# Combining the experts' outputs: rows sorted by token tile through an indirect store, 15 cells in place of 64 dense blocks

## The chip, the cores and the metric

The kernel runs on one core of one Trainium2 chip. The metric is device time in microseconds (us), the median of three runs. One further execution was recorded by the hardware profiler; every duration below comes from that execution.

## The reference, cut to what matters

The program is two transformer layers on 1024 tokens of width 256: attention and a low-rank mixture in layer 0, grouped attention, a shared expert and a routed mixture of 32 experts in layer 1. The change lies in the routed mixture at the end. In the reference (the wrapping removed):

```python
oh = one_hot(sel, E)                          # 1024 tokens x 4 choices, E = 32 experts
pos = (cumsum(oh, axis=0) * oh).sum(-1) - 1   # place of the choice within its expert
valid = pos < CAP                             # CAP = 32: an expert takes its first 32 tokens
xe = zeros((E, CAP, h)).at[sel, posc].add(x[tok] * valid[:, None])
g = silu(einsum('ech,ehf->ecf', xe, Wg)); u = einsum('ech,ehf->ecf', xe, Wu)
ye = einsum('ecf,efh->ech', g * u, Wd)        # 32 x 32 rows of 256
y_pair = ye[sel, posc] * (w * valid)[:, None]
out = shared.at[tok].add(y_pair)              # each row is added to its token
```

So there are 1024 slot rows of 256 values, and each is added, with its weight, to one of 1024 tokens. The layer's result is the residual X plus the attention's projection, the shared expert times a sigmoid gate, and these rows.

## The kernel before

**Engines and queues.** Each engine has its own program, written by hand, and waits on semaphores. In the last 65 us the order of the work on TensorE (PE), ScalarE (ACT) and VectorE (DVE) is the list `EXPERT_STEPS` (line 33): each engine walks the same list and does its own share of each step. GpSimd (POOL) and the queue of SyncE (SP) have orders of their own.

**Steps.** The 32 experts are 8 groups g of 4, so that a group has 128 slots. `("slots", g)` transposes the gathered token rows and ACT copies them. `("up", g)` makes both hidden halves in 16 matmuls, ACT applies silu (line 928), and DVE multiplies (line 1937) into `HE`. `("turn", g)` transposes `HE` on PE and ACT copies it to `HTE` (lines 933 and 934). `("down", g)` makes the group's 128 output rows in bank 7, and DVE copies them to `YE` (line 1940). `("sd", j)` is the shared expert's down projection of token tile j (8 tiles of 128 tokens); from tile 4 on it runs in three float32r matmuls for each product, high by low, low by high and high by high (lines 965 to 967). It needs the low parts `SDl` and `ACTl`, which DVE makes in the `("split", n)` steps (lines 1945 and 1948). `add_shared(j)` on DVE (line 1915) adds a tile to X.

**Attention of layer 1.** POOL multiplies the small attention's probabilities by the values, 32 operations of 128x256 for the eight tiles (lines 648 and 652), while the steps run. PE then transposes the result in 16 transposes (line 1446), ACT and DVE split it into high and low, and `mix_proj(j)` multiplies it by the projection, 6 matmuls for a tile.

**The combination.** `slot_mask(g)` on DVE (line 1906) compares the 1024 token numbers with the token of each of the group's 128 slots: a 128x1024 matrix of zeros and ones. ACT scales `YE` by the slots' weights into `YH` (line 911) and DVE makes the remainder `YL` (line 1910). `mix_groups(j, groups, ...)` on PE (lines 1407 and 1408) multiplies, for token tile j and each of the 8 groups, a 128x128 block of the mask by `YH` and by `YL`: 64 blocks, 128 matmuls. Tiles 0 to 3 take groups 0 to 5 within the steps ("mix", 0 to 3), as fillers between up, turn and down of group 7; the rest follows after `("down", 7)`. DVE adds each tile to X (line 1921) and SP stores it (line 525).

**Gathering.** The slots' tokens come from a table that PE, DVE and ACT build; POOL then fetches token rows by eight indirect transfers (line 638), one for each group. SP brings the experts' weights, 4 places for 8 groups.

## Time and profile before

| | us |
|---|---|
| median of 3 runs | 430.81 (430.78 to 430.83) |
| the profiled execution, its own time | 429.98 |
| its span, first to last instruction | 427.7 |
| PE busy | 422.6 (99%) |
| DVE busy | 311.3 (73%) |
| ACT busy | 248.8 (58%) |
| POOL busy | 169.2 (40%) |

How to read it: the span is what the hardware profiler saw between the first and the last instruction of the core; the execution's own time is 2.28 us more, around the span. Engines work at the same time, so that their busy times overlap. A busy PE is one with a matmul in flight, and its matmuls overlap too: the start-to-start distance is what one costs.

### The profile page before, as it was taken

What the parts mean: (1) busy time and instruction counts of PE and PEld (TensorE: products, weight loads), DVE (VectorE), ACT (ScalarE), POOL (GpSimd) and SP (SyncE); (2) the same over time, 40 slices, a digit from 0 to 9 for tenths busy, and PEclk for the clock granted to TensorE, in tenths of its full rate; (3) what the DMA queues carried; (4) which work ended last, traced back from release to release, by engine and by line L of the source; (5) the groups of instructions that cost most, each with busy time, mean ns of one, the idle gap of its engine ahead of it and who ended that gap; (6) DMA issues with size and microseconds to landing.
All of it is one profiled execution on the core that took longest, in us unless ns stands there. A gap on an engine that the chain in (4) does not pass through costs nothing.

```text
span 427.7 us, 8922 instructions
## 1 busy us (share of the span) xinstructions
PE 422.6 (99%) x3096; PEld 380.7 (89%) x3096; DVE 311.3 (73%) x913; ACT 248.8 (58%) x676; POOL 169.2 (40%) x293
## 2 busy tenths in 40 slices
PE   8999999999999999999999999999999999999997
PEld 8888889999999999999999999999997777567897
DVE  5967576787787988887877776748589995588442
ACT  4666651886868788787868687433414622463120
POOL 3232001655455455545455530101167106799100
PEclk9999999999999999999999999999999999999999
DMA  6740011501010101010000000000099952999002
GB/s 206 182 130 2 0 51 49 196 3 51 2 51 0 51 3 49 2 33 20 2 2 2 2 2 2 25 14 14 14 295 298 306 153 75 246 306 280 7 14 86
DMA packets 42026, 34.45 MB, mean 81 GB/s; under 512 B 6736, under 2 KB 40192, under 8 KB 41984
## 3 DMA queue, kind: packets, MB, share of 16 engines
q1 hardware_dynamic: 41600, 32.85, 27.1%
q0 software_dynamic: 384, 1.05, 0.9%
q8 instruction: 25, 0.41, 0.4%
q14 instruction: 17, 0.14, 0.1%
HBM read 31.80 MB, written 2.10 MB: 79 GB/s over the span
## 4 chain that ended last, share of the span: by engine, by line
PE 98%; ACT 1%; issue 0%; DVE 0%; POOL 0%; POOLq 0%; DVEq 0%
PE bank L965 22%; PE bank L966 22%; PE bank L967 22%; PE bank L1163 5%; PE bank L1175 3%; PE bank L1154 3%; PE bank L1396 2%; PE bank L1363 2%; PE bank L1407 2%; PE bank L1383 2%; PE bank L1408 2%; PE bank L1205 2%; PE bank L1053 1%; PE bank L1312 1%; PE bank L1015 1%; PE bank L1351 1%
## 5 line engine op out<-in xcount | busy, mean ns | idle before, releaser
L601 POOL TENSOR_TENSOR arena<-arena,rinv 128x384 f32<-128x384 f32 x64 | 52.9, 827 | 81.2 <-DVE rinv L1680 81.2
L965 PE MATMUL bank<-XTl,WA 128*128 128x512 f32 (+1 forms) x126 | 51.9, 412 | 0.0
L967 PE MATMUL bank<-XTh,WA 128*128 128x512 f32 (+1 forms) x126 | 49.1, 390 | 0.0
L966 PE MATMUL bank<-XTh,WA 128*128 128x512 f32 (+1 forms) x126 | 49.1, 389 | 0.0
L791 ACT ACTIVATE PT<-bank 128x256 fp32r<-128x256 f32 x64 | 24.4, 381 | 34.2 <-PE bank L1163 34.1
L1684 DVE TENSOR_TENSOR PT<-bank,PT 128x256 fp32r<-128x256 f32 x64 | 27.2, 425 | 18.8 <-ACT arena L792 18.7
L965 PE MATMUL bank<-WA,XTh 128*128 128x256 f32 x128 | 38.3, 299 | 0.0
L966 PE MATMUL bank<-WA,XTl 128*128 128x256 f32 x128 | 35.7, 279 | 0.0
L967 PE MATMUL bank<-WA,XTh 128*128 128x256 f32 x128 | 35.7, 279 | 0.0
L592 POOL CAST Q<-arena 128x128 fp32r<-128x128 f32 x64 | 18.6, 290 | 37.6 <-PE bank L967 37.6
L1672 DVE CUSTOM_DVE_ANT_0 arena<-bank,posm 128x128 f32<-128x128 f32 x64 | 18.1, 283 | 20.9 <-PE bank L967 20.8
L784 ACT ACTIVATE arena<-arena,nmax 128x256 f32<-128x256 f32 x64 | 32.4, 505 | 0.0
L594 POOL TENSOR_TENSOR Q<-arena,Q 128x128 fp32r<-128x128 f32 x64 | 29.5, 462 | 5.1
L1163 PE MATMUL bank<-ident,arena 128*128 128x128 f32 x192 | 31.4, 272 | 0.0
L797 ACT ACTIVATE arena<-bank,VC 128x256 f32<-128x256 f32 x64 | 30.0, 469 | 0.1
L967 PEld LDWEIGHTS bank<-XTh,WA 128*128 128x128 f32 x126 | 23.7, 188 | 5.3
L965 PEld LDWEIGHTS bank<-XTl,WA 128*128 128x128 f32 x126 | 23.8, 189 | 3.8
L966 PEld LDWEIGHTS bank<-XTh,WA 128*128 128x128 f32 x126 | 23.8, 189 | 3.8
L1674 DVE CUSTOM_DVE_ANT_0 arena<-bank,posm 128x256 f32<-128x256 f32 x64 | 26.9, 420 | 0.0
L782 ACT ACTIVATE arena<-arena,nmax 128x128 f32<-128x128 f32 x64 | 25.9, 405 | 1.5 <-DVE nmax L1674 1.1
L694 ACT ACTIVATE arena<-bank,bqs 128x512 f32<-128x512 f32 x16 | 18.4, 1152 | 14.0 <-PE bank L967 13.2
L1545 DVE TENSOR_SCALAR arena<-bank,bqs 128x512 f32<-128x512 f32 x16 | 17.2, 1098 | 12.7 <-PE bank L967 12.7
(345 smaller groups left out, 1471.2 us busy)
## 6 DMA issues: line engine op xcount, KB each, us to landing
arena<-in_L_ffn_Wg SPq DMA_DIRECT2D x6, 704.0 KB, 7.9
arena<-in_L_ffn_Wu SPq DMA_DIRECT2D x6, 704.0 KB, 10.1
arena<-in_L_ffn_Wd SPq DMA_DIRECT2D x6, 512.0 KB, 7.4
arena<-in_L_attn_Wk SPq DMA_DIRECT2D x8, 256.0 KB, 2.6
arena<-in_L_attn_Wv SPq DMA_DIRECT2D x8, 256.0 KB, 3.5
arena<-in_L_attn_Wo SPq DMA_DIRECT2D x1, 2048.0 KB, 9.2
arena<-in_L_ffn_Wd SPq DMA_DIRECT2D x6, 192.0 KB, 7.4
arena<-in_L_attn_Wq SPq DMA_DIRECT2D x4, 256.0 KB, 4.5
```

Of the source, the lines that this page charges most:

```text
L594: pool.tensor_tensor(QL[:, u % 3], q, QH[:, u % 3].bitcast(F32), ALU.subtract).then_inc(s_qh, 1)
L601: pool.tensor_tensor(pr, pr, r[:, :, None].to_broadcast([P, 3, P]), ALU.mult).then_inc(s_p, 1)
L782: nc.scalar.activation(Pb[i][:, 0:128], Pb[i][:, 0:128], ACT.Exp, bias=nmax[:, i, 0:1], scale=-1.0, accum_out=psumr[:, i, 0:1])
L784: nc.scalar.activation(Pb[i][:, 128:384], Pb[i][:, 128:384], ACT.Exp, bias=nmax[:, i, 1:2], scale=-1.0, accum_out=psumr[:, i, 1:2]).then_i ...
L791: nc.scalar.activation(PTH[:, u % 2], pb[2 + u % 2][:, 0:256], ACT.Copy)
L797: nc.scalar.activation(QO[:, h, b], pb[4 + u % 2][:, 0:256], ACT.Identity, bias=VC[:, 32 + h:33 + h]).then_inc(s_Oc, 1)
L965: pe.matmul(dst, wh, xl, start=start, stop=False)
L966: pe.matmul(dst, wl, xh, start=False, stop=False)
L967: return pe.matmul(dst, wh, xh, start=False, stop=stop)
L1163: ins = pe.transpose(pb[2 + u % 2][:, P * i:P * i + P], Pb[u % 3][:, P * i:P * i + P], ident[:])
L1674: nc.vector.tensor_tensor_reduce(Pb[i][:, 128:384], bank[:, 128:384], MASK, -1.0, -MASKED, ALU.add, ALU.min, nmax[:, i, 1:2]).then_inc(s_m, 1)
L1684: nc.vector.tensor_tensor(PTL[:, u % 2], pb[2 + u % 2][:, 0:256], PTH[:, u % 2].bitcast(F32), ALU.subtract).then_inc(s_Tl, 1)
```

## The change

The combination is replaced. Each slot row is given a rank: its place in an order of all slots by token tile (first all slots whose token is in tile 0, then tile 1, ...). DVE works the ranks out in four parts, `ranks(0)` to `ranks(3)`, from counts that PE makes beside the positions. ACT writes the weighted rows with the token's number as a 257th column (`YW`); POOL stores the rows of each group to a table in DRAM by an indirect store (eight "scatters"); SP loads the table back in four transfers once all eight are there. In the sorted table, block g of 128 rows and token tile j meet only along a staircase of 15 cells. For each cell i, DVE works out the tokens and makes one 128x128 mask, and PE runs two matmuls (high and low) whose bank and block are addressed by a register, loaded from `tile_of` by `value_load`. What else moves: the 8 masks of 128x1024 and the steps "mix", "high" and "low" go; DVE does tile 7 of the attention's values (`last_values`) and POOL only tiles 0 to 6, with scatters 0 to 3 ahead of tile 6; the attention's transposes come before down 7, and shared-down 6 and 7 after it; the projection starts its own sums; ACT, not DVE, empties bank 7; the zeroing of the table's first half is a 1 MB store by SP early on. Counting on PE: 16 wider matmuls in place of 36.

```diff
-                 ("mask", (4, 5)), ("split", 0), ("weigh", 0), ("down", 2), ("turn", 3), ("split", 1), ("split", 2), ("sd", 2),
-                 ("split", 3), ("down", 3),
+                 ("ranks", 0), ("split", 0), ("weigh", 0), ("down", 2), ("turn", 3), ("split", 1), ("split", 2), ("sd", 2),
+                 ("ranks", 1), ("split", 3), ("down", 3),
                  ("up", 4), ("slots", 5), ("split", 4), ("sd", 3), ("split", 5), ("turn", 4), ("split", 6), ("up", 5), ("slots", 6),
-                 ("mask", (6,)), ("down", 4), ("mask", (0,)), ("sd", 4), ("mask", (1, 2)), ("turn", 5),
-                 ("mask", (3,)), ("sd", 5), ("mask", (7,)), ("down", 5),
-                 ("high", 0), ("up", 6), ("slots", 7), ("high", 3), ("low", 0), ("sd", 6), ("turn", 6), ("low", 3),
-                 ("sd", 7), ("add", 7), ("down", 6), ("mix", 0), ("mix", 1), ("up", 7), ("mix", 2), ("turn", 7),
-                 ("mix", 3), ("down", 7)]
+                 ("ranks", 2), ("down", 4), ("sd", 4), ("ranks", 3), ("turn", 5), ("values", 0), ("sd", 5), ("down", 5),
+                 ("up", 6), ("slots", 7), ("values", 1), ("add", 5), ("turn", 6), ("down", 6), ("up", 7), ("ao", 1),
+                 ("turn", 7), ("ao", 0), ("down", 7), ("sd", 6), ("sd", 7), ("add", 6), ("add", 7)]
...
+DONE = {3: 0, 8: 1, 9: 2, 10: 3, 11: 4, 12: 5, 13: 6, 14: 7}
+PV_STEPS = [("values", j) for j in range(6)] + [("scatter", g) for g in range(4)] + [("values", 6)] + [("scatter", g) for g in range(4, GR)]
...
+            sp.dma_start(sorted_rows[0:N].rearrange("(g p) d -> p g d", p=P), ZR[:, None, :].to_broadcast([P, GR, ROW])).then_inc(s_xs, 16)
...
+            for g in range(GR):
+                sp.wait_ge(s_xg[g], 32)
+            for k in range(B):
+                sp.dma_start(YS[:, 2 * k:2 * k + 2], sorted_rows[2 * P * k:2 * P * k + 2 * P].rearrange("(g p) d -> p g d", p=P)).then_inc(s_x[k], 16)
...
+                if what == "scatter":
+                    if n == 0:
+                        pool.wait_ge(s_rk, 1)
+                    pool.wait_ge(s_ye, n + 1)
+                    pool.indirect_dma_start(sorted_rows, bass.IndirectOffsetOnAxis(ap=rank[:, n:n + 1], axis=0), YW[:, n], None).then_inc(s_xg[n], 16)
+            for g in range(1, GR, 2):
...
+                pool.tensor_tensor(y_part(g, 1), YS[:, g, 0:D], y_part(g, 0).bitcast(F32), ALU.subtract).then_inc(s_pv, 1)
...
+                if what == "down":
+                    act.wait_ge(s_dn, n + 1)
+                    act.wait_ge(s_sw1, 1)
+                    nc.scalar.activation(YW[:, n, 0:D], pb[7][:, 0:D], ACT.Copy, scale=slot_w[:, n:n + 1])
+                    nc.scalar.activation(YW[:, n, D:ROW], slot_t[:, n:n + 1], ACT.Copy).then_inc(s_ye, 1)
...
+            for g in range(GR):
+                act.wait_ge(s_x[g // 2], 32)
+                nc.scalar.activation(y_part(g, 0), YS[:, g, 0:D], ACT.Copy).then_inc(s_yr, 1)
...
-            for j in range(NT):
-                for i in range(j + 1):
-                    ins = pe.matmul(pb[6][:, E1 * j:E1 * j + E1], (trib if i == j else onesb)[:], selb[:, i],
+            for i in range(NT):
+                pe.matmul(pb[6][:, 256 + E1 * i:512].rearrange("p (j e) -> p j e", e=E1), onesb[:],
...
             def shared_down(j):
...
+                    if j == 4:
+                        pe.wait_ge(s_rk, 2)
...
                 for m in range(FC):
+                    if j >= 4 and len(tiles) < CELLS:
+                        tiles.append(pe.value_load(tile_of[0:1, len(tiles):len(tiles) + 1], min_val=0, max_val=NT - 1))
...
-                for g in groups:
-                    pe.matmul(dst, GT[g][:, ts], YH[:, g], start=start and g == groups[0], stop=False)
-                    ins = pe.matmul(dst, GT[g][:, ts], YL[:, g], start=False, stop=stop and g == groups[-1])
...
+            def values_turn(half):
+                if half == 1:
+                    pe.wait_ge(s_pd, 1)
+                    pe.wait_ge(s_pv, 25)
...
+            def cell(i):
+                pe.wait_ge(s_dm, NT + i + 1)
+                if i < GR:
+                    pe.wait_ge(s_yl, i // 2 + 1)
+                    if i % 2:
+                        pe.wait_ge(s_pv, 25 + i // 2 + 1)
+                dst = banks[:, bass.ds(tiles[i], 1), 0:D].rearrange("p a n -> p (a n)")
+                for low in range(2):
+                    rows_of = YX[:, CELLS - 1 - i:CELLS - 1 - i + NT, D * low:D * low + D]
+                    ins = pe.matmul(dst, MS[:, i], rows_of[:, bass.ds(tiles[i], 1)].rearrange("p a n -> p (a n)"),
+                                    start=False, stop=False, skip_group_check=True)
...
+            def ranks(part):
...
+                    step(nc.vector.tensor_scalar(CS[:, 1:NT + 1], TOT[:], float(CAP), None, ALU.min))
+                    step(nc.vector.tensor_tensor(SUMS[0][:, :, 16:48], CS[:, 1:NT + 1], CS[:, 0:NT], ALU.subtract))
+                    nc.vector.tensor_reduce(RS, CS, AX, ALU.add)
+                    for k in range(5):
+                        old, new, by = SUMS[k % 2], SUMS[1 - k % 2], 1 << k
+                        step(nc.vector.tensor_tensor(new[:, :, 16:48], old[:, :, 16:48], old[:, :, 16 - by:48 - by], ALU.add))
...
+                    nc.vector.tensor_copy(rank[:], T8).then_inc(s_rk, 1)
...
+                    nc.vector.tensor_copy(tile_of[:, 0:CELLS], JJ).then_inc(s_rk, 1)
...
+            def cell_tokens(i0, i1, groups):
...
+                for i in range(i0, i1):
+                    nc.vector.tensor_scalar(MS[:, i], IT, tok[:, i:i + 1], None, ALU.is_equal).then_inc(s_dm, 1)
...
+            y_low(0)
+            y_low(2)
+            cell_tokens(0, 4, 4)
+            y_low(4)
             y_low(6)
+            cell_tokens(4, CELLS, GR)
             for j in range(NT):
                 add_rest(j)
```

Of `ranks`, part 0 has 4 memsets and 8 operations of 256 to 288 columns, part 1 six of 256 and two of 4, part 2 eight of 8 to 64 (it ends in `rank`), part 3 seven of 7 to 105 up to `tile_of` and three more.

## Rows read from the trace of the kernel before

**Rows 1.** The page's head and part 1: busy us, share, instructions.

```profile
span 427.7 us, 8922 instructions
PE 422.6 (99%) x3096; PEld 380.7 (89%) x3096; DVE 311.3 (73%) x913; ACT 248.8 (58%) x676; POOL 169.2 (40%) x293
```

**Rows 2.** The page's part 4, the chain that ended last, by engine.

```profile
PE 98%; ACT 1%; issue 0%; DVE 0%; POOL 0%; POOLq 0%; DVEq 0%
```

**Rows 3.** Lines 1407 and 1408: ns min/median/max, first and last start us.

```profile
L1407 PE MATMUL bank<-YH,GT x64: 278/283/386, 399.3 to 421.2; 128*128 128x256 f32 x64
L1408 PE MATMUL bank<-OS,GT x64: 274/282/285, 399.6 to 421.3; 128*128 128x256 f32 x64
```

**Rows 4.** Timeline of PE: start us, us, engine, line, operation, tiles, form.

```profile
383.64 0.27 PE L1373 MATMUL bank<-ident,arena 128*128 128x128 f32 x1
...
386.64 0.39 PE L965 MATMUL bank<-SDl,ACTh 128*128 128x256 f32 x1
...
388.87 0.27 PE L1373 MATMUL bank<-ident,arena 128*128 128x128 f32 x1
...
407.00 1.07 PE L1383 MATMUL bank<-WAF,arena 128*32 128x256 f32 x16
408.00 1.97 PE L1446 MATMUL bank<-ident,arena 128*128 128x128 f32 x16
...
424.81 0.27 PE L967 MATMUL bank<-PJ,AOTh 128*128 128x256 f32 x1
```

**Rows 5.** Timeline of DVE; in brackets the idle time before and its releaser.

```profile
336.27 0.42 DVE L1824 TENSOR_TENSOR tmp<-tmp,sel 128x256 f32<-128x256 f32 x1
336.72 0.42 DVE L1825 TENSOR_REDUCE ws<-tmp 128x8 f32<-128x256 f32 x1
...
353.21 0.23 DVE L1887 TENSOR_SCALAR idx<-bank 128x4 uint32<-128x4 f32 x2
...
353.43 0.18 DVE L1895 TENSOR_TENSOR slot_p<-bank,slot_e 128x32 f32<-128x32 f32 x1
...
372.53 2.13 DVE L1906 TENSOR_SCALAR GT<-FRF,slot_t 128x1024 fp32r<-128x1024 f32 x2
374.59 2.20 DVE L1945 TENSOR_TENSOR SDl<-FRF,SDh 128x1536 fp32r<-128x1536 f32 x1
...
385.04 0.75 DVE L1948 TENSOR_TENSOR ACTl<-arena,ACTh 128x512 fp32r<-128x512 f32 x1 [1.12 <-ACT ACTh L945]
385.75 0.34 DVE L1937 TENSOR_TENSOR arena<-arena,bank 128x176 f32<-128x176 f32 x1
386.01 0.83 DVE L1906 TENSOR_SCALAR GT<-FRF,slot_t 128x1024 fp32r<-128x1024 f32 x1
...
425.19 0.42 DVE L1921 TENSOR_TENSOR X<-bank,X 128x256 f32<-128x256 f32 x1 [0.28 <-PE bank L967]
```

**Rows 6.** Line 525, SP's last stores: ns to issue one; us to landing.

```profile
L525 SPq DMA_DIRECT2D out<-X x8: 332/333/362, 415.0 to 425.6; - x8
```

**Rows 7.** Timeline of ACT.

```profile
389.29 0.28 ACT L933 ACTIVATE arena<-bank 128x128 f32<-128x128 f32 x1 [3.16 <-PE bank L1374]
...
408.60 0.51 ACT L911 ACTIVATE YH<-arena,slot_w 128x256 fp32r<-128x256 f32 x1 [2.49 <-DVE arena L1940]
```

**Rows 8.** Timeline of POOL: the first gather.

```profile
354.31 1.14 POOL L638 DMA_INDIRECT arena<-token_rows,idx  x1 [21.28 <-DVE idx L1887]
```

**Rows 9.** The page's part 6: issues, KB each, median us to landing.

```profile
arena<-in_L_attn_Wk SPq DMA_DIRECT2D x8, 256.0 KB, 2.6
arena<-in_L_attn_Wv SPq DMA_DIRECT2D x8, 256.0 KB, 3.5
...
arena<-token_rows,idx POOLq DMA_INDIRECT x8, 2.7
```

**Rows 10.** Windows: us, busy of the engines (x), granted PE clock, DMA share, GB/s.

```profile
427.00:427.70 0.70, 0.00 (x0) 0.00 (x0) 0.00 (x0) 0.00 (x0) 0.00 (x0) 0.61 0.00 0
```

**Rows 11.** The chain in order of time, the old counting: start us, us, line.

```profile
332.52 0.91 PE bank L1302 x36
```

More of the change, by code:

```diff
@@ L70, in sem @@
             return ctx.enter_context(nc.semaphore(name))
-        pb = [ctx.enter_context(nc.psum_tensor(f"bank{i}", [P, 512], F32)) for i in range(8)]
+        banks = ctx.enter_context(nc.psum_tensor("banks", [P, 8, 512], F32))
+        pb = [banks[:, i] for i in range(8)]
         ident = sb("ident", [P, P])
@@ L249, in program @@
         pvt = sb("pvt", [P, 256])
-        s_x = [sem(f"x_loaded{b}") for b in range(B)]
+        s_x = [sem(f"x_then_sorted_rows_loaded{b}") for b in range(B)]
         s_xb0 = sem("x_second_tile_loaded")
@@ L896, in _ @@
             nc.scalar.activation(SCp[0], SCp[0], ACT.Exp, scale=SCALE1).then_inc(s_ae, 1)
+            act.wait_ge(s_pm, 1)
+            nc.scalar.activation(TOT[:], pb[6][:, 256:512].rearrange("p (j e) -> p j e", j=NT), ACT.Copy)
             silu(3)
@@ L1465, in _, with proj @@
-            for j in range(4, NT):
-                mix_proj(j)
+                if what == "ao":
+                    values_turn(n)
+            def proj(j):
+                ts = slice(P * j, P * j + P)
+                for c in range(C):
+                    ins = mm3(pb[j][:, 0:D], AOTh[:, c, ts], AOTl[:, c, ts], PJh[:, c], PJl[:, c], c == 0, c == C - 1)
+            pe.wait_ge(s_pjl, 1)
+            pe.wait_ge(s_al, 4)
+            pe.wait_ge(s_eh, GR)
+            pe.wait_ge(s_ec, GR)
+            pe.wait_ge(s_ye, GR)
@@ L1469, in _ @@
+            for i in range(CELLS):
+                cell(i)
         @block.vector
@@ new lines, in last_values @@
+            def last_values(part):
+                j = NT - 1
+                if part == 0:
+                    dve.wait_ge(s_ap, 2)
+                for k in (0, 1) if part == 0 else (2, 3):
+                    dst = AO[:, j] if k == 0 else pvt2
+                    p, v = value_operands(j, k)
+                    step(nc.vector.tensor_tensor(dst.rearrange("p (g r d) -> p g r d", g=G1, r=4), p, v, ALU.mult))
+                    if k:
+                        ins = nc.vector.tensor_tensor(AO[:, j], AO[:, j], pvt2, ALU.add)
+                        if k == 3:
+                            ins.then_inc(s_pd, 1)
+                        else:
+                            step(ins)
@@ L1950, in _ @@
                     scores_weighed(1)
-                if what == "mask":
-                    for g in n:
-                        dve.wait_ge(s_it, 4)
-                        slot_mask(g)
-                if what == "low":
-                    for g in range(n, n + 3):
-                        y_low(g)
-                if what == "sd" and n >= 1:
+                if what == "ranks":
+                    ranks(n)
+                if what == "values":
+                    last_values(n)
+                if what == "ao":
+                    if n == 1:
+                        dve.wait_ge(s_pjh, 1)
+                        nc.vector.tensor_tensor(PJl[:], projT[:], PJh[:].bitcast(F32), ALU.subtract).then_inc(s_pjl, 1)
+                    for c in range(C):
+                        xs = slice(512 * n, 512 * n + 512)
+                        dve.wait_ge(s_ac, 2 * (1 - n) + c + 1)
+                        nc.vector.tensor_tensor(AOTl[:, c, xs], pb[ao_bank(c, n)][:], AOTh[:, c, xs].bitcast(F32), ALU.subtract).then_inc(s_al, 1)
+                if what == "sd" and 1 <= n < 6:
                     add_shared(n - 1)
```

232 lines of the change are left out of this document (141 added, 91 removed).

## The prediction

> **What bounds the kernel now.** I read the page first: PE is busy for 99% of the span [rows 1], and the chain that ended last is PE for 98% of it [rows 2]. So what PE is spared is worth its full length, as long as PE then has something else to do. What one matmul costs is read from starts, not from lengths, since matmuls overlap: shared-down of tile 4, 18 matmuls of 256 columns, runs from 386.64 to 388.87 [rows 4], 0.12 us each, while one is listed at 0.28. The combination has 128 such matmuls [rows 3]: 15.4 us of PE. The timeline of PE then shows where they lie: 48 ahead of the end of down 7 (408.00), 80 behind it, between the attention's transposes and the last matmul, which ends at 425.08 [rows 4]. Then I read DVE's timeline, because the change gives DVE work in the middle of the steps: between 372.53 and 386.01 it has one gap, 1.12 us [rows 5]. The last addition ends at 425.61 and the span at 427.7: 2.1 us for the last store [rows 5]. The sum is made against this execution (span 427.7, own time 429.98); its own time is 0.83 us under the median of the runs, so a difference in the span is added to 430.81.
>
> **What PE is spared.** 30 matmuls in place of 128: 98 times 0.12 us, 11.8 us. If nothing else changed, the span would be 416. The rest of the text is where this goes.
>
> **DVE ahead of shared-down 4.** In the new order PE may not start ("sd", 4) until `tile_of` is there, the end of `ranks(3)`'s seventh operation; before, it started at 386.64. DVE's list up to there: from 372.53 to the end of HE(5) at 386.01 are 13.48 us. Taken away: masks 4 and 5 (2.06 us, up to the start of `SDl`), two copies out of bank 7 (0.37 each, a little under the 0.42 of a like operation), the gap of 1.12, since DVE is no longer the one that waits; 9.56 us stay [rows 5]. A third copy that is gone, ahead of 372.53, lets it start at 372.2. Added: a step of 256 columns that waits for the one before it costs 0.45 us, start to start, a small one 0.21 (0.18 and its wake-up) [rows 5]. `ranks(0)`: eight of the former and four memsets of 0.1, 4.0 us; `ranks(1)`: six and two, 3.1 us. POOL multiplies the attention's values meanwhile: two masks took 1.03 us each in this stretch, one later 0.83 or less [rows 5]. So the 7.1 us are worth between 7.1 and 8.9 (times 1.25); I take times 1.2, 8.5 us, near the row of the same stretch. HE(5) is then done at 390.3; `ranks(2)` is 8 small steps, 1.7 us; the addition of tile 3 is 0.4; seven small steps of `ranks(3)` are 1.5. `tile_of` comes at 393.9: shared-down 4 starts 7.3 us late (5.5 to 7.8). Queued behind PE's wait are turn 5, shared-down 5 and all of groups 6 and 7. Half of the lateness shows earlier: HE(4) stands behind both `ranks` in DVE's list, so turn 4, which ran at 383.64 [rows 4], comes near 387.4.
>
> **From shared-down 4 to the end of down 7.** Before: 386.64 to 408.00, 21.36 us [rows 4]. Out go shared-down 6 and 7 (4.5 us) and 48 matmuls (5.8 us): 11.1 stay. In come 16 transposes, 1.7 us (1.97 less the last one's tail [rows 4]). The removed work was also cover. Before turn 6 PE now waits for silu and the multiplication, 0.1 + 0.3 + 0.34 with only the 0.2 of slots 7 beside it: 0.6; before down 6 for ACT's two copies, which start 0.42 after the turn (388.87 to 389.29) and take 0.43 together, less the turn itself: 0.7; before down 7 for ACT, which has the attention's copies in hand: 0.3 [rows 4, 5, 7]. That is 1.6 us.
>
> **Register loads.** PE does 12 `value_load`s in this stretch, one ahead of each three matmuls (0.37 us). No row shows one. Below: 0, if the sequencer works ahead and the matmuls in its queue hide it, which they cannot for the first after a wait. Above: 0.87 each, what POOL took from DVE's idx (353.44) to the start of its first transfer (354.31) [rows 5, 8]. The nearest row is the sequencer's work for one transfer on SP, 0.33 us [rows 6], less than the three matmuls that follow; I take 0.08 each to be seen, 1.0 us in all. By the Trainium skill, "DMA: Bandwidth & Descriptors", section "Latency and other measured facts", a `tensor_load` has a floor of about 600 ns; no run shown here has one. By that figure 12 loads would be 7.2 us in place of 1.0 if nothing hid them (an estimate from that page).
>
> So the end of down 7 is 393.9 + 11.1 + 1.7 + 1.6 + 1.0 = 409.3, 1.3 us later than before, although 10.3 us of PE work ahead of it are gone.
>
> **The chain behind down 7.** It is new, and each link waits for the one before. ACT's weighted copy and the token column: 0.51 and 0.2 [rows 7]. POOL's wake to an indirect transfer 0.87 [rows 5, 8], and the transfer 2.7 to landing as the gathers had; bounds 2.1 (the last store of 128 KB [rows 5]) and 3.5 [rows 9]. SP then loads four times 263 KB: like the pairs of 256 KB, 2.6 for the first and 1.3 more for the next (3.5, issued 0.4 later) [rows 9]. ACT's first high part 0.5. To here 7.4 us: 416.7. Now DVE, in its order: low part 0 (0.45), a wait for the second load (0.7), low part 2 (0.4), three small steps (0.6), four masks of 128x128 (0.2 each by size, 0.8), two low parts (0.8), three steps of up to 88 columns (0.75), eleven masks (2.2), the last cell (0.3), eight additions back to back (0.38 each, 3.0): 10.0 us, all from steps of 0.42 to 0.45 for 256 columns and 0.2 for small ones [rows 5]. Then 2.1 for the last store. End: 428.8. Meanwhile PE does shared-down 6 and 7 (4.5) and 48 projection matmuls (5.8), from 409.3 to 419.6, about when the first cells can start: this is the cover of the chain, and it ends before the chain does. The cells' register addresses, four a cell, have no row either: between 0 and 0.3 us a cell (0.33, [rows 6]); as the masks come every 0.2 us, I take 0.3 in all.
>
> **Small parts.** The counting: 36 matmuls in 0.91 us [rows 11] become 16 with twice the columns, 2304, 1.1 us at 0.12 for 256: +0.2. At nothing: the zeroing store, the three small POOL operations and ACT's copy of the totals; early on, DMA queues and POOL have idle stretches beside a PE that never stops, and if that cover were gone the store would cost its own few us once. POOL's scatters 0 to 3 start once `rank` is there, about 392.4, 1.3 us each (1.14 [rows 8] and its issue); values of tile 6 follow until about 404, just ahead of the transposes that wait for them; this costs nothing, and 1 us for each 0.25 us more a scatter.
>
> **Sum.** 428.8 + 0.3 + 0.2 = 429.3 against 427.7: +1.6 us. Median 430.81 + 1.6 = 432.4.
>
> **The rivals.** The forecast (A): the saving is spent on DVE's lateness (7.3), lost cover and the chain; 432.4, its own range 430.5 to 434.3. Chance 0.37.
>
> B, faster: DVE is less late. If the 256-column steps of `ranks` run at the 0.3 us of a one-input operation's rate (a mask of 1024 columns in 0.83 [rows 5]) or POOL does not slow them, `tile_of` comes 3 us sooner, and everything behind it moves with it: 426.3, median 429.4. It decides from 1.6 us on. For it: the chain from `tile_of` to the end has no slack, so each us counts. Against it: these steps have two inputs, like the 0.45 row. Chance 0.36.
>
> C, the clock: PE idles some 3.5 us before turn 4 and 3.6 before shared-down 4. In the trace the granted clock is 1.00 all along and falls to 0.61 on average in the last 0.7 us, some 2 us after PE's last matmul at 425.08 [rows 4, 10], so it can fall from the upper level (2.4 GHz) to the lower (1.2) in such a gap. If it does ahead of shared-down 4, its 2.2 us double: 434.6. The Trainium skill, "TensorE: Matmul & The Clock Gate", section "What's actually happening", says that the gate's default is throttled and that activity releases it; the last window agrees. Chance 0.15.
>
> D, the register loads are not hidden at all: 12 times 0.37 (0.33 [rows 6] and a wake-up) rather than 0.08, 3.5 us more: 435.9. For it: after its wait PE's queue is empty. Against it: 0.33 is less than the three matmuls behind each load. The Trainium skill's floor of a `tensor_load`, in the page and section named above, speaks for D. Chance 0.12.
>
> **How the numbers follow.** About 0.2% (0.9 us) is what a measurement of this kernel can tell from no change. B lies faster for 0.32 of its 0.36, the rest within; A lies within for 0.12 of its 0.37 and slower for 0.25; C and D are slower. Faster 0.32, same 0.16, slower 0.52. The low end takes B and adds loads and cells at 0 and DVE unhindered: 429.4 less 1.0, 0.3 and 1.4, 426.7, rounded to 426.5; the high end takes D, a scatter that lands at 3.5 (0.8) and DVE at times 1.25 (0.4): 437.1, to 437.5. Some 0.1 lies outside on either side.
>
> **What would show it.** PE idle ahead of turn 4 and of shared-down 4, the latter ended by DVE's `tile_of` near 394; the gaps between shared-down 4's threes 0.12 (loads hidden) or more; down 7 ending near 409; the last scatter landing 4.3 us behind it; DVE without a gap of more than 1 us from the first low part to the last addition; a granted clock of 1.00 through 395. The forecast is wrong if `tile_of` comes before 392, if the tail behind down 7 is under 17 us or over 22, or if the clock falls.

## The result, and the profile after

The changed kernel takes 437.87 us (437.73 to 438.28, 4 runs) where the kernel before takes 430.82 (430.78 to 431.82, 4 runs): a ratio of 1.0163 [1.0151, 1.0174], 7.0 us slower. The forecast was 432.4, its range ended at 437.5. The profiled execution of the changed kernel took 438.28 us around a span of 436.5; the working forecast a span of 429.3.

The page's head, part 1 (busy us, share, instructions) and the shares of the chain that ended last, changed kernel:

```profile
span 436.5 us, 8871 instructions
PE 418.3 (96%) x2978; PEld 371.0 (85%) x2978; DVE 317.3 (73%) x959; ACT 252.3 (58%) x693; POOL 171.1 (39%) x301
PE 87%; DVE 6%; DMA 2%; ACT 2%; issue 1%; SPq 0%; DVEq 0%
```

PE (TensorE) runs 118 matmuls fewer (98 in the combination, 20 in the counting), and its share falls from 99 to 96%: the chain is no longer PE alone [rows 1, 2]. Where PE idles is seen in its timeline (start us, us, engine, line, operation; in brackets the idle time before and its releaser):

```profile
383.68 0.59 PE L1468 MATMUL banks<-FRF,arena 128*128 128x256 f32 x2
388.47 0.48 PE L1437 MATMUL banks<-ident,arena 128*128 128x128 f32 x1 [4.20 <-DVE arena L2079]
...
389.09 2.58 PE L1427 MATMUL banks<-arena 128*32 128x352 f32 x16
...
392.21 1.78 PE L1447 MATMUL banks<-arena 128*32 128x256 f32 x16
397.55 0.57 PE L1027 MATMUL banks<-SDl,ACTh 128*128 128x256 f32 x1 [3.56 <-issue]
...
402.83 0.38 PE L1027 MATMUL banks<-SDl,ACTh 128*128 128x256 f32 x1
...
403.50 0.38 PE L1027 MATMUL banks<-SDl,ACTh 128*128 128x256 f32 x1
...
414.57 1.07 PE L1447 MATMUL banks<-WAF,arena 128*32 128x256 f32 x16
416.55 0.38 PE L1027 MATMUL banks<-SDl,ACTh 128*128 128x256 f32 x1 [0.91 <-DVE AOTl L2101]
...
428.79 3.77 PE L1531 MATMUL banks<-YX,MS 128*128 x22 [0.52 <-DVE MS L2048]
```

PE's timeline shows two long gaps, ahead of turn 4 (388.47) and of shared-down 4 (397.55); threes of shared-down that start 0.67 us apart (402.83, 403.50) instead of 0.37; and down 7 (414.57) ending near 415.6, against 408.0 before [rows 4]. From there to the end of the span are 20.9 us.

DVE's timeline, which says what shared-down 4 waited for:

```profile
374.24 3.70 DVE L1990 TENSOR_TENSOR arena<-arena 128x256 f32<-128x256 f32 x5
...
383.94 0.83 DVE L1996 TENSOR_TENSOR arena<-arena,slot_e 128x256 f32<-128x256 f32 x1
384.81 0.42 DVE L1997 TENSOR_REDUCE arena<-arena 128x64 f32<-128x256 f32 x1
385.26 0.42 DVE L1998 TENSOR_TENSOR arena<-arena,slot_e 128x256 f32<-128x256 f32 x1
...
388.08 0.33 DVE L2079 TENSOR_TENSOR arena<-arena,banks 128x176 f32<-128x176 f32 x1
...
392.08 0.34 DVE L2079 TENSOR_TENSOR arena<-arena,banks 128x176 f32<-128x176 f32 x1 [1.21 <-ACT arena L989]
...
395.99 0.17 DVE L2021 CAST tile_of<-arena 128x15 uint32<-128x15 f32 x1
```

`tile_of` is there at 396.16. Shared-down 4 starts 1.37 us after it, and its idle time is put down to "issue": that 1.37 is the first register load, in front of an empty queue. And the windows (start:end, length, busy of PE, PEld, DVE, ACT, POOL, then granted clock, DMA share, GB/s):

```profile
382.00:386.00 4.00, 2.27 (x11) 1.66 (x9) 3.83 (x8) 1.69 (x5) 2.34 (x3) 1.00 1.16 312
386.00:390.00 4.00, 1.53 (x10) 0.62 (x14) 3.83 (x11) 0.81 (x3) 0.00 (x0) 0.61 1.14 267
390.00:394.00 4.00, 3.99 (x30) 1.08 (x22) 2.45 (x10) 0.84 (x3) 0.00 (x0) 0.54 1.17 318
394.00:398.00 4.00, 0.45 (x2) 0.46 (x3) 3.62 (x16) 0.56 (x2) 2.39 (x3) 0.89 0.75 211
398.00:402.00 4.00, 3.83 (x20) 3.36 (x19) 0.16 (x2) 0.00 (x0) 3.51 (x5) 0.68 0.28 97
402.00:416.00 14.00, 12.14 (x121) 7.07 (x120) 5.82 (x13) 6.07 (x19) 5.80 (x8) 1.00 0.09 31
```

The granted clock falls to the lower level (1.2 GHz) behind each of the two gaps: up 5, the 16 matmuls at 389.09, takes 2.58 us, and behind the gaps a matmul takes 0.21 us where it took 0.12.

### The profile page after: what moved, and what is told of

Its sections match the earlier page's. It is cut to its first block, busy times and chain, and to the rows that moved or that the text cites. A ratio compares the mean times of both kernels' runs of the same rounds, so it can differ in the third digit from the quotient of the medians.

```text
span 436.5 us, 8871 instructions
## 1 busy us (share of the span) xinstructions
PE 418.3 (96%) x2978; PEld 371.0 (85%) x2978; DVE 317.3 (73%) x959; ACT 252.3 (58%) x693; POOL 171.1 (39%) x301
## 4 chain that ended last, share of the span: by engine, by line
PE 87%; DVE 6%; DMA 2%; ACT 2%; issue 1%; SPq 0%; DVEq 0%
PE banks L1027 22%; PE banks L1029 21%; PE banks L1028 21%; PE banks L1225 5%; PE banks L1237 3%; PE banks L1216 3%; PE banks L1427 2%; PE banks L1267 2%; DMA arena<-sorted_rows 1%; PE banks L1447 1%; PE banks L1531 1%; DMA arena<-in_L_attn_Wq 1%; PE banks L1377 1%; DVE arena L1990 1%; PE banks L1077 1%
## 5 line engine op out<-in xcount | busy, mean ns | idle before, releaser
L1027 PE MATMUL banks<-XTl,WA 128*128 128x512 f32 (+1 forms) x126 | 51.9, 412 | 0.0
L1029 PE MATMUL banks<-XTh,WA 128*128 128x512 f32 (+1 forms) x126 | 49.1, 390 | 0.0
L1028 PE MATMUL banks<-XTh,WA 128*128 128x512 f32 (+1 forms) x126 | 49.1, 390 | 0.0
L854 ACT ACTIVATE PT<-banks 128x256 fp32r<-128x256 f32 x64 | 24.5, 383 | 34.1 <-PE banks L1225 34.0
L1756 DVE TENSOR_TENSOR PT<-banks,PT 128x256 fp32r<-128x256 f32 x64 | 27.2, 425 | 18.8 <-ACT arena L855 18.8
L1027 PE MATMUL banks<-WA,XTh 128*128 128x256 f32 x128 | 38.3, 299 | 0.0
L1028 PE MATMUL banks<-WA,XTl 128*128 128x256 f32 x128 | 35.7, 279 | 0.0
L1029 PE MATMUL banks<-WA,XTh 128*128 128x256 f32 x128 | 35.7, 279 | 0.0
L1225 PE MATMUL banks<-ident,arena 128*128 128x128 f32 x192 | 31.4, 272 | 0.0
L860 ACT ACTIVATE arena<-banks,VC 128x256 f32<-128x256 f32 x64 | 30.0, 469 | 0.1
L1029 PEld LDWEIGHTS banks<-XTh,WA 128*128 128x128 f32 x126 | 23.7, 188 | 5.4
L1028 PEld LDWEIGHTS banks<-XTh,WA 128*128 128x128 f32 x126 | 23.8, 189 | 3.8
L1746 DVE CUSTOM_DVE_ANT_0 arena<-banks,posm 128x256 f32<-128x256 f32 x64 | 26.9, 420 | 0.0
```

The costliest lines, as they stand in the source:

```text
L854: nc.scalar.activation(PTH[:, u % 2], pb[2 + u % 2][:, 0:256], ACT.Copy)
L860: nc.scalar.activation(QO[:, h, b], pb[4 + u % 2][:, 0:256], ACT.Identity, bias=VC[:, 32 + h:33 + h]).then_inc(s_Oc, 1)
L1027: pe.matmul(dst, wh, xl, start=start, stop=False)
L1028: pe.matmul(dst, wl, xh, start=False, stop=False)
L1029: return pe.matmul(dst, wh, xh, start=False, stop=stop)
L1225: ins = pe.transpose(pb[2 + u % 2][:, P * i:P * i + P], Pb[u % 3][:, P * i:P * i + P], ident[:])
```

## The experiments

So three things that the forecast kept apart came at once: DVE (VectorE) still later than said (A's mechanism), loads that are not hidden (D), a clock that falls (C). They overlap in one stretch, and the trace alone does not price them. The theories under test: the loads set the pace of shared-down; the clock does; DVE's lateness is the root, through the place of `ranks` in its list; or, as the rival, the round trip of the rows through DRAM at the end. The ratios are to the kernel before, measured beside each.

**Constants for the tile numbers.** No load and no register address; PE still waits for `tile_of`.

```diff
-            tiles = []
+            tiles = [0, 0, 0, 0, 1, 1, 1, 1, 1, 2, 3, 4, 5, 6, 7]
...
-                    if j >= 4 and len(tiles) < CELLS:
-                        tiles.append(pe.value_load(tile_of[0:1, len(tiles):len(tiles) + 1], min_val=0, max_val=NT - 1))
```

> The 15 tile numbers are written as constants for these inputs, so the 15 register loads and the register-addressed operands of the cells go; PE's wait for tile_of ahead of shared-down 4 stays. Loads theory (a load is work of PE's sequencer, some 0.65 us, and sets the pace of shared-down 4 and 5): the 1.37 us between tile_of and shared-down 4 goes, and 12 threes fall from 0.65 to 0.75 us apart to 0.36, a little more where the granted clock is 0.50: 3.6 to 5 us off, 433 to 434.3. Rival (the loads are hidden as the forecast had it, and the wait for DVE and the chain behind down 7 carry the loss): at most 1 us off, 436.8 to 437.9.

434.71 us, 1.0083 [1.0066, 1.0099]: 3.2 us below the changed kernel. PE's timeline:

```profile
396.17 0.35 PE L1027 MATMUL banks<-SDl,ACTh 128*128 128x256 f32 x1 [2.17 <-DVE tile_of L2019]
...
396.60 0.28 PE L1027 MATMUL banks<-SDl,ACTh 128*128 128x256 f32 x1
...
397.59 0.42 PE L1029 MATMUL banks<-SDh,ACTh 128*128 128x256 f32 x1
397.81 0.42 PE L1027 MATMUL banks<-SDl,ACTh 128*128 128x256 f32 x1
...
425.03 2.89 PE L1529 MATMUL banks<-YX,MS 128*128 128x256 f32 x22 [1.11 <-DVE MS L2046]
```

Shared-down 4 starts with `tile_of`, not 1.37 later, and its threes are 0.43 apart at first. Then the clock falls, 0.21 or 0.22 a matmul from 397.6 to 400.8: some 16 matmuls at 0.095 more are 1.5 us, a loss that the loads had covered. The last 22 matmuls of the cells take 2.89 in place of 3.77, at a granted clock of 1.00 in both: with register addresses 0.17 each, with constants 0.13. The edit takes out loads and addresses together, so the 3.2 us are the price of both.

**The loads alone, in the kernel before.** 12 loads at the same places of shared-down 4 and 5; their values go nowhere.

```diff
+                    pe.wait_ge(s_ix, 1)
+                    if j in (4, 5):
+                        pe.value_load(idx[0:1, m:m + 1], min_val=0, max_val=N)
```

> The kernel before, with 12 register loads added, one ahead of each three matmuls of shared-down 4 and 5, from a table that has long been ready; nothing uses the numbers. Loads theory (each holds PE's sequencer for some 0.65 us beside 0.36 us of matmuls): the threes of shared-down 4 and 5 start 0.65 to 0.7 us apart in place of 0.35, and the time rises by 12 times 0.3 to 0.35, 3.5 to 4.2 us, to 434.5 to 435.2. Rival (hidden, as the forecast's 0.08 each had it): 1 us more at most, 430.8 to 432.

434.53 us, 1.0080 [1.0064, 1.0097], +3.5. The granted clock is 1.0 all through and nothing waits for DVE here, so the loads have this price by themselves. PE's timeline:

```profile
387.61 0.38 PE L965 MATMUL bank<-SDl,ACTh 128*128 128x256 f32 x1 [0.33 <-issue]
...
388.28 0.38 PE L965 MATMUL bank<-SDl,ACTh 128*128 128x256 f32 x1
...
388.94 0.38 PE L965 MATMUL bank<-SDl,ACTh 128*128 128x256 f32 x1
```

Threes every 0.66 to 0.67 us, from a sequencer that gets through one load in that time.

**A load ahead of every second three.** Shared-down 4 to 7, turn 6, down 6 and turn 7 share the fifteen.

```diff
-                    if j >= 4 and len(tiles) < CELLS:
+                    if j >= 4 and m % 2 == 1:
+                        load_tile()
+                if (what, n) in (("turn", 6), ("down", 6), ("turn", 7)):
+                    load_tile()
```

> The same 15 loads, but one ahead of every second three of shared-down 4 to 7 and one each ahead of turn 6, down 6 and turn 7, so that some 0.72 us of matmuls lie between two loads. If the sequencer takes a load beside the matmuls that PE still has queued, so that only a load closer than 0.65 us behind the last one shows: shared-down 4 and 5 take 2.2 to 2.8 us each, and the time is 2.5 to 4 us less than 437.9, so 434 to 435.4. If a load stops PE for its own length wherever it stands: nothing is won, 437.5 to 438.5, and shared-down 6 and 7 behind down 7 are 1.8 us longer.

435.27 us, 1.0093 [1.0075, 1.0111]: 2.6 us back. In shared-down 5, at full clock, every second three has a load ahead and none shows:

```profile
401.84 0.31 PE L1027 MATMUL banks<-SDl,ACTh 128*128 128x256 f32 x1
...
402.23 0.28 PE L1027 MATMUL banks<-SDl,ACTh 128*128 128x256 f32 x1
...
402.58 0.28 PE L1027 MATMUL banks<-SDl,ACTh 128*128 128x256 f32 x1
```

So a load is hidden by 0.7 us of matmuls, and not by 0.37.

**PE kept busy in the two gaps.** 36 transposes ahead of turn 4 and 40 ahead of shared-down 4, into a free part of a bank.

```diff
+                if g == 4:
+                    pe.wait_ge(s_ec, g)
+                    keep_busy(36)
...
+                        keep_busy(40)
```

> Adds 36 transposes of the identity into an unused part of bank 6 ahead of the wait of turn 4 and 40 ahead of the wait of shared-down 4, so that PE has no gap there; nothing reads them. Clock theory of the forecast (the fall of the clock costs shared-down 4 its 2.2 us once more): granted clock 1.00 from 386 to 401, 2.2 us off and 1.2 more from up 5 (2.58 us against 1.39) that DVE's ranks(2) waits for behind HE(5): 434.3 to 435. Loads theory: the threes of shared-down 4 stay 0.65 us apart with the clock at 1.00, since the loads set them; only up 5's 1.2 us comes back: 436.5 to 437. If the clock matters nowhere, 437.9.

437.48 us, 1.0147 [1.0130, 1.0164]: 0.4 below the changed kernel. The clock did stay up, in every window, and the threes did not come closer:

```profile
394.00:398.00 4.00, 3.87 (x31) 3.38 (x29) 2.65 (x10) 0.00 (x0) 3.09 (x4) 1.00 0.92 249
```
```profile
396.83 0.38 PE L1027 MATMUL banks<-SDl,ACTh 128*128 128x256 f32 x1
...
397.51 0.39 PE L1027 MATMUL banks<-SDl,ACTh 128*128 128x256 f32 x1
```

The clock is not what sets the time while the loads do: threes are 0.66 to 0.68 apart at either clock. `tile_of` came at 394.98, 1.2 earlier than in the changed kernel (up 5 took 1.39 again), which is what the lower clock did to DVE's lateness. In the trace that reached the end, with a span of 435.3 for 436.5; the medians of the times differ by 0.4 only.

**`ranks(1)` behind the multiplication of group 5.**

```diff
-                 ("ranks", 1), ("split", 3), ("down", 3),
+                 ("split", 3), ("down", 3),
-                 ("ranks", 2), ("down", 4), ("sd", 4), ("ranks", 3), ("turn", 5),
+                 ("ranks", 1), ("ranks", 2), ("down", 4), ("sd", 4), ("ranks", 3), ("turn", 5),
```

> Only DVE's order is changed: ranks(1) stands behind HE(5) in place of behind the addition of tile 1, so HE(4) no longer waits for it. Theory (what counts is all of DVE's work ahead of tile_of, not which of PE's waits it lands in): turn 4 comes 3.5 to 4 us sooner and the gap ahead of it goes; tile_of comes 1.5 to 2.5 us sooner, since ranks(1) then runs beside an idle POOL and fills DVE's 1.2 us wait for silu(5); the gap ahead of shared-down 4 grows to some 5 us; time 435.4 to 436.4. Rival (each gap of PE is a loss of its own): the 4.2 us ahead of turn 4 come back whole, 433.7.

436.88 us, 1.0136 [1.0119, 1.0152], slower than both theories gave: turn 4 comes at 385.35, but PE's gap ahead of shared-down 4 grows to 7.66. The gap only moved; the same work stands ahead of `tile_of`, which comes at 394.75, 1.4 sooner. DVE's first step of the moved `ranks(1)`, then PE:

```profile
387.78 0.42 DVE L1993 TENSOR_TENSOR arena<-arena 128x256 f32<-128x256 f32 x1
```
```profile
396.14 0.57 PE L1027 MATMUL banks<-SDl,ACTh 128*128 128x256 f32 x1 [7.66 <-issue]
```

Where it stands now POOL idles, and the same `ranks(1)` takes 3.1 us (387.78 to 390.91) in place of 4.0.

**No wait for the rows' round trip.** Rows are loaded from another table.

```diff
-            for g in range(GR):
-                sp.wait_ge(s_xg[g], 32)
+            sp.wait_ge(s_ye, GR)
```

> The loads of the sorted rows read a table of zeros that nothing is scattered into, and start once ACT has written the last YW; the scatters are still issued. Left out is the experts' part of the output. If the round trip behind down 7 sets the end: the loads start 3 to 3.5 us sooner, the projection's last matmul is then what the cells wait for, and the time falls by as much as the masks allow, 1.5 to 3 us, to 435 to 436.4. If PE's own work behind down 7 (shared-down 6 and 7 with three loads, the projection, the cells) sets it, under 1 us: 437 to 437.9.

436.88 us, 1.0138 [1.0121, 1.0155]: 1.0 below, between the two ranges that were expected. With the last store's 2.95 us taken out of the chain, PE's own work behind down 7 (shared-down 6 and 7, the projection) stands next in it, and the cells follow that without a gap:

```profile
426.67 3.76 PE L1534 MATMUL banks<-YX,MS 128*128 x30
```

So the round trip is worth 1.0 us of the 7.0, and the rival falls as the main cause. The line also limits the reading of the cells above: here all 30 matmuls with register addresses take 0.12 each. They took 0.17 where they follow DVE's masks, so it is not the price of such an address as such.

**Constants and no wait for `tile_of`.** As the first, without `pe.wait_ge(s_rk, 2)`.

> As the run with constant tile numbers (434.7), and PE's wait for tile_of ahead of shared-down 4 goes too. The gap of 4.2 us ahead of turn 4 stays. If DVE's lateness at shared-down 4 is a loss beside the one at turn 4: shared-down 4 starts at the end of down 4, near 393.4 in place of 396.2, and is no longer behind a gap, but runs at the lower clock that the first gap leaves; 2 to 2.8 us off, 431.9 to 432.7. If something further on is late anyway (scatters, transposes of tile 6, the multiplication for turn 6): under 1 us off.

433.38 us, 1.0056 [1.0039, 1.0073], between the two ranges that were expected: shared-down 4 follows down 4 at once (393.20 for 396.17 with constants), and down 7 still ends 3.0 sooner (408.86 for 411.92). Only 1.9 of it reach the end in the traces (spans 431.3 and 433.2) and 1.3 in the medians. A late signal shows in two places of ACT's timeline:

```profile
401.03 0.47 ACT L1010 ACTIVATE arena<-banks,slot_w 128x256 f32<-128x256 f32 x1 [4.73 <-remote]
...
410.18 0.47 ACT L1010 ACTIVATE arena<-banks,slot_w 128x256 f32<-128x256 f32 x1 [1.48 <-PE banks L1447]
```

At the first it waits for down 5, whose last matmul was over at 398.95. The semaphore's event comes 2.1 us later, behind POOL's first four scatters, issued 1.28 us apart from 395.2 to 400.1; what that costs is made up by down 7, since shared-down runs at the upper clock here. At the second it sees the end of down 7 1.3 late, beside the next scatters. The rest is lost at the end: behind a gap of 1.15 us the last 22 matmuls take 4.19 us in place of 2.89, at a granted clock of 0.65.

**The work in another order.** `ranks(1)` late, `ranks(3)` near the end, POOL's seven tiles of values ahead of all scatters, loads behind down 7.

```diff
-PV_STEPS = [("values", j) for j in range(6)] + [("scatter", g) for g in range(4)] + [("values", 6)] + [("scatter", g) for g in range(4, GR)]
+PV_STEPS = [("values", j) for j in range(7)] + [("scatter", g) for g in range(GR)]
...
-                    if j == 4:
+                    if j == 6:
                         pe.wait_ge(s_rk, 2)
```

> Same work as the change, placed otherwise: ranks(1) behind HE(5), values of tile 7 behind HE(6), ranks(3) behind the attention's copies, no wait for tile_of at shared-down 4, POOL's values of tile 6 ahead of the scatters, and the 15 loads behind down 7, one for every second three of shared-down 6 and 7 and one for each tile of the projection. Theory (the loss is the placing: DVE ahead of turn 4 and shared-down 4, the loads' pace, the clock that falls in the gaps): PE's gaps ahead of turn 4 and shared-down 4 are under 1 us each, the granted clock stays at 1.00 from 382 to 402, down 7 ends near 403 in place of 415.6, the tail behind it stays 20 to 21.5 us; 424 to 427, under the kernel before. Rival (the scatters, 1.28 us each from 394 on, or the contention of POOL's values with DVE's ranks, take the place of the stalls): down 7 ends near 403 to 406 but the last scatter is issued behind 407; 428 to 432.

432.60 us, 1.0049 [1.0033, 1.0064], above both ranges that were expected. Shared-down 4 starts at 388.60 and the clock stays up to 402, yet the end does not follow: seven scatters are now issued back to back, 1.28 us apart, and silu of group 7, whose matmuls ended at 399.5, starts at 402.62. A variant in which POOL also does half of tile 7's products and `ranks(3)` comes ahead of turn 6:

> As the run called reordered (432.6), with the two things mended that its trace shows as late: ranks(3) up to tile_of stands ahead of turn 6 in DVE's list in place of behind the attention's copies (there it came at 409.8 and PE waited 2.40 for it at the lower clock), and POOL, idle for 3.9 us ahead of the first scatter, does the first two of tile 7's products. Theory (the work fits, only its places were wrong): no wait for tile_of, the granted clock 1.00 up to 403 at least, down 7 ends near 403, scatters every 1.28 us from 395.4 on, the last one issued near 404.5, 425 to 427.5. ACT stood still from 399.54 to 402.62 in that run with nothing on the chip left to wait for; if that comes again at the same place (instructions that it has not got yet), turn 7 is 2.5 us late, the clock may fall behind it, and the time is 428 to 430.

432.23 us, 1.0034 [1.0020, 1.0048], and the same stall:

```profile
403.08 0.32 ACT L989 ACTIVATE arena<-banks 128x176 f32<-128x176 f32 x1 [3.81 <-remote]
```

**What makes the signal late?** Two further variants of that kernel: 40 more waits on ACT, already fulfilled, ahead of its first silu (if ACT's own instruction supply were the cause, the stall would move); and twice the space for the indirect transfers' descriptors, 4096 bytes for 2048.

> As reordered2, with 40 waits that are long fulfilled added in ACT's list ahead of silu of group 0, where ACT is idle for over 4 us; they take no part in the computation. If ACT's stop of 3.08 us near 400 is a fetch of its next block of instructions (the queue of instruction transfers shows one packet of 8 KB that begins at 399.75 and takes 0.88 us where others take 0.35), the block's end moves by up to 40 instructions and the stop goes or lands elsewhere: 1 to 2.5 us away from reordered2 in either direction, and no stop at silu(7). If the stop belongs to the work (a wait that the trace does not name), both runs show it at the same instruction and agree within 0.5 us.

> As reordered2 (432.2), with twice the space for the indirect transfers' descriptors (4096 bytes in place of 2048), for which four small tiles lie elsewhere. In reordered2 the signal of up 7's end, 399.43, was seen at 403.06, and those of the attention's transposes, 400.01, at 405.88, while POOL issued seven scatters 1.28 us apart; otherwise they come 0.01 to 0.04 us after the end. If the late signals come of POOL waiting for room behind the scatter before: the scatters start 1.0 us apart, the signals are late by under 0.5 us, ACT does not stand still at silu(7): 426 to 428.5. If they come of the scatters as such: same lateness, 431.5 to 432.8.

432.83, 1.0045 [1.0028, 1.0061], and 432.55, 1.0045 [1.0031, 1.0060]: silu of group 7 at 403.37 and 403.11, the scatters 1.28 us apart as before. Neither moves the stall. Then seven indirect stores at the end of POOL's list in the kernel before, which nothing reads:

```diff
+            for g in range(7):
+                pool.indirect_dma_start(extra, bass.IndirectOffsetOnAxis(ap=plain[:, g:g + 1], axis=0), SD[:, 0], None).then_inc(s_xg[0], 16)
```

> The kernel before, with seven indirect stores of 128 rows of 1 KB added at the end of POOL's list, from a constant tile into a table that nothing reads; POOL is idle there and nothing waits for them. If indirect stores that follow each other hold up PE's completion signals by themselves: between 398.5 and 408 signals of PE come 1 to 4 us late, silu(7) or turn 7 with them, and the time rises by 1 to 3 us, 431.8 to 434. If the late signals belong to the changed program (its order, its register loads): none late by over 0.3 us, and the time stays within 0.4 us of 430.9.

435.47 us, 1.0116 [1.0095, 1.0137], +4.5, more than expected. Up 7's matmuls end at 405.03, ACT sees it at 408.38. ACT, then PE, then the window behind the gap:

```profile
408.40 0.32 ACT L936 ACTIVATE arena<-bank 128x176 f32<-128x176 f32 x1 [7.00 <-remote]
```
```profile
409.14 0.33 PE L1381 MATMUL bank<-ident,arena 128*128 128x128 f32 x1 [2.49 <-DVE arena L1945]
```
```profile
410.00:414.00 4.00, 4.00 (x30) 2.51 (x29) 0.82 (x2) 0.77 (x3) 0.00 (x0) 0.58 0.02 4
```

Adding indirect stores in a row is enough to make PE's signal late in a kernel that has nothing else of the change, and the lower clock follows the gap.

**`ranks` early, nothing else moved.** In the changed kernel DVE idles from 361.7 to 366.2, ahead of the first group's multiplication (HE(0)).

```diff
-                 ... ("sd", 0), ("up", 0), ...
+                 ... ("sd", 0), ("ranks", 0), ("up", 0), ("slots", 2), ("up", 1), ("turn", 0), ("slots", 3), ("up", 2),
+                 ("ranks", 1), ("down", 0), ("turn", 1), ("slots", 4), ("up", 3), ("ranks", 2), ("down", 1), ...
```

> From the changed kernel, only ranks(0), ranks(1) and ranks(2) are moved to the same early places as in early_ranks; ranks(3), the wait for tile_of at shared-down 4 and the 12 loads in shared-down 4 and 5 stay. If the placing of DVE's work is the largest part of the loss: turn 4 follows without a gap, tile_of comes near 389, shared-down 4 waits some 1.5 us for it and the first load, the threes stay 0.65 us apart; 4.5 to 6.5 us off the changed kernel, 431.4 to 433.4, so that the loads' places account for the other 2 to 4 us up to early_ranks. If DVE's lateness was only one of several waits that end together, 1 to 3 us off: 435 to 437.

431.08 us, 0.9999 [0.9990, 1.0008]: 6.8 us off by placing alone, and better than the range expected of it. No gap at turn 4 is left; at shared-down 4 there is one:

```profile
389.81 0.38 PE L1027 MATMUL banks<-SDl,ACTh 128*128 128x256 f32 x1 [2.57 <-issue]
```

**`ranks` early and the loads behind down 7**, so that shared-down 4 waits for nothing; and, in a second kernel, the attention's transposes ahead of up 7 as well.

```diff
+                    if j == 6:
+                        pe.wait_ge(s_rk, 2)
+                        load_tile()
+                    if j >= 6 and m % 2 == 1:
+                        load_tile()
```
```diff
-                 ("down", 6), ("up", 7), ("ao", 1), ("turn", 7), ("ao", 0), ("down", 7),
+                 ("down", 6), ("ao", 1), ("ao", 0), ("up", 7), ("turn", 7), ("down", 7),
```

> From the changed kernel: ranks(0) to where DVE waits 4.5 us for silu of group 0 (361.7 to 366.2), ranks(1) behind HE(2) and ranks(2) behind HE(3), so that rank is there near 377 in place of 394; ranks(3) stays ahead of the values of tile 7; no wait for tile_of at shared-down 4, the 15 loads behind down 7 as in reordered. POOL keeps its order: values 0 to 5, four scatters, values 6, four scatters, so no more than four scatters follow each other closely and they start near 385, when PE's signals of groups 5 to 7 are still to come. Theory (placing of DVE's work and of the scatters made the loss): turn 4 and shared-down 4 each follow without a gap of over 1 us, granted clock 1.00 to the end of the cells, down 7 ends near 402 and the tail takes 20.5 to 21.5 us: 423.5 to 426. Rival (PE's completion signals are late by 1 to 3 us wherever scatters follow each other, as in the reordered runs, or DVE's ranks delay HE(0) to HE(3) as much as they did HE(4)): 428 to 432.

> As early_ranks (429.55), with the attention's 16 transposes and their copies ahead of up 7 in place of around turn 7. In early_ranks PE stood still for 2.42 us ahead of up 7, for the weights of group 7 (landed near 399.7), and the clock fell behind it. If what is left there is that wait and the transposes can fill it: the gap falls under 1 us, the clock stays at 1.00, down 7 ends 1.5 to 2 us sooner, near 404, and the time is 427 to 428.3. If the transfers or PE's late signals set this stretch anyway: within 0.5 us of early_ranks.

429.55 us, 0.9971 [0.9958, 0.9984], then 428.14 (427.23 to 429.10), 0.9926 [0.9910, 0.9942]: the last is 2.8 us below the kernel before and 9.7 below the changed one. The first of the two came out in its rival's range (428 to 432). DVE and PE of the last, whose profiled execution is its slowest (429.10):

```profile
363.99 2.26 DVE L1997 TENSOR_TENSOR arena<-arena 128x256 f32<-128x256 f32 x5
```
```profile
385.08 0.27 PE L1437 MATMUL banks<-ident,arena 128*128 128x128 f32 x1
...
398.65 3.54 PE L1486 MATMUL banks<-ident,arena 128*128 128x128 f32 x16 [0.66 <-issue]
...
405.30 1.07 PE L1447 MATMUL banks<-WAF,arena 128*32 128x256 f32 x16 [0.52 <-ACT arena L995]
```

Down 7 is done by 406.4, ahead of the kernel before, although the clock still falls once: the 16 transposes at 398.65 take 3.54 us, at a granted clock of 0.53. In the first of the two, PE waits 2.42 us for group 7's weights ahead of up 7, and 1.04 behind down 7 for the low part of the attention's rows:

```profile
399.77 1.62 PE L1427 MATMUL banks<-arena 128*32 128x352 f32 x16 [2.42 <-DMA arena<-in_L_ffn_Wu]
```

In the second the transposes fill the former wait, and the latter is gone. Yet down 7 ends at 405.9 in the first one's trace, so the traces do not show what the 1.4 us between the two medians are made of.

## Why the prediction was wrong

The sign and the mechanism were right: what PE is spared is spent on DVE's lateness, lost cover and a chain at the end. The size was off, by terms treated as exclusive rivals that came together. By spans, the error is 436.5 - 429.3 = 7.2 us:

- **DVE ahead of shared-down 4: `tile_of` at 396.2, not 393.9 (+2.3).** The step that failed is "I take times 1.2". `ranks(0)` and `ranks(1)` took 5.5 and 4.0, 9.5 us for 8.5. The five scan steps, two inputs of 256 columns, took 0.74 each while POOL multiplied, and the same steps 0.45 each in the last kernel, where POOL does not; that is 1.64 times, above the upper bound of 1.25, which had come from masks with one input. Moved beside an idle POOL, `ranks(1)` took 3.1, the forecast's value without a factor. The second step that failed took the wait ahead of HE(5), the multiplication of group 5, out of the list, "since DVE is no longer the one that waits": it waited 1.21 there, and with PE held at the upper clock, so that up 5 took 1.39 in place of 2.58, `tile_of` came 1.2 sooner. Some 0.2 of the 2.3 were there before `ranks`: DVE's list started at 372.44, not 372.2. The range given for the lateness, 5.5 to 7.8, is 5.8 to 7.6 by its own terms; 9.5 were measured to `tile_of`. Of B, which hoped for less, nothing came.
- **Loads and clock, from `tile_of` to the end of down 7: 19.4 us, not 15.4 (+4.0).** "0.33 is less than the three matmuls that follow" failed: a load takes 0.66, or 1.37 in front of an empty queue. With constants the stretch was 15.9 (396.0 to 411.9), some 1.5 of it the lower clock's; the remaining 14.4 are what was forecast without loads. With PE kept busy it was 18.9 (395.0 to 413.8), loads and no lower clock: the loads so cost 4.5 here, where 1.0 was forecast; D had these 4.5 in all. The last 0.5 is the lower clock beside them. The Trainium skill, "DMA: Bandwidth & Descriptors", section "Latency and other measured facts", gives a `tensor_load` a floor of about 600 ns; the 0.66 agrees, and that floor was a better guide than SP's row.
- **C, the clock.** It fell, as C said, but 2.2 us were not added: held up, it gave back 0.4 in the medians and 0.5 in this stretch. While the loads set the pace of shared-down, the lower clock does not show there; with the loads gone it cost 1.5. A sum of 432.4, C's 2.2 and D's 3.5 would be 438.1, near the measured 437.87, but the parts of it are not those: DVE is 2.3 of them.
- **The tail: 20.9, not 20.0 (+0.9)**, inside the 17 to 22 given; the 20.0 hold the 0.2 for the counting, which did not show. The last 22 matmuls of the cells took 0.17 each where those with constants took 0.13: 0.9 us, where 0.3 was forecast. The round trip was worth only 1.0.
- **What PE is spared** was right: 98 matmuls went. Turn 4 was late at the place forecast, and 1.1 more: 388.5 for 387.4, by the same excess of `ranks`.

The difference of medians, 7.0, is smaller than that of the two profiled spans, 8.8, because the execution profiled before lies 0.83 under its median and the one after 0.41 over, and 2.28 and 1.78 us lie around the spans. The placing of `ranks` is the largest part: 6.8 us came back with it alone, more than the 2.3 by which it was misjudged, because the forecast had accepted the other 7 us of lateness as the price of the change. The parts don't add: loads and addresses gave 3.2 us when constants took their place, and moving the loads gave 1.5 once `ranks` was early.

## What to carry to other kernels

A chain of small dependent steps goes where its engine idles, not where its result is first read: the three `ranks` take 11.3 us in the changed kernel (5.5, 4.0, 1.8) and 11.4 in the last one (3.8, 4.2, 3.4), and only there do they stand off the path. The gain came from the place, not from faster steps. Read register values in a stretch where each has 0.7 us of queued work behind it, and not first thing after a wait. When two rivals start from the same gap, give their joint occurrence a chance; the range was too short because C and D were counted as alternatives.

## What the runs showed of the hardware

PE's completion signals were seen late while POOL issued indirect transfers back to back (1.25 to 1.28 us apart). In the trace of before, a signal is seen 0.04 us or less after its matmul, also beside the eight gathers; with seven scatters added up 7's was 3.35 late, and in the reordered kernel's variant two were 3.6 and 5.9 late. Not every signal beside such transfers is late, and the trace of before is the exception for the first silu: in every other trace, of the kernel before with additions too, its signal comes 1.3 to 1.6 us late beside the eight gathers. ACT in the kernel before with the 12 loads, where up 0 ended at 364.52:

```profile
365.94 0.32 ACT L928 ACTIVATE arena<-bank 128x176 f32<-128x176 f32 x1 [4.52 <-PE bank L1363]
```

So some 0.5 us of the changed kernel's lateness (turn 2 at 372.13 for 371.66) is not the change's doing: it comes from the one execution of before that the forecast was measured against. In the trace with 40 more waits on ACT, fulfilled ones too stopped twice, for 1.2 and 1.4 us, between 361.7 and 364.3, so it is not PE's signal alone. Doubling the descriptors' space and shifting ACT's instructions changed nothing; the cause was not found.

DVE's steps with two inputs of 256 columns took 0.45 us beside an idle POOL and 0.74 while POOL multiplied; masks with one input took 0.83 and 1.03. A register load on PE took 0.66 us in a row and 1.37 in front of an empty queue.
